# Mixture-of-experts layer on one core: the first block's normalisation on VectorE, unread products around its transposes, setup copies of ScalarE moved, the last turn reordered and stored in halves

## The reference, cut to what matters

```python
xn = layernorm(x)                                   # x: 16 x 512 x 128
q, k, v = xn @ q_w, xn @ k_w, xn @ v_w              # 32 channels
attn = ((q @ k.T) * decay_weights) @ v @ o_w.T * out_scale
logits = xn @ router_w + router_b + load_balancer; rw, sel = softmax(top_2(logits))
e0 = silu(xn @ sw_w1) * (xn @ sw_w3) @ sw_w2
e1 = gelu(sym @ me_c1w + me_c1b) @ me_c2w + me_c2b  # sym: three linear maps of xn
h2 = layernorm(syn + attn_ce); ff = relu(h2 @ f1w + f1b) @ f2w + f2b
e2 = layernorm(h2 + ff) @ gen_w + gen_b
e3 = gelu(xn @ ml_w1 + b) @ ml_w2 + b
out = x + attn + sum(rw * the two experts of sel)
```

## Time and profile before

| | |
|---|---|
| time, median of 3 runs | 475.91 us (475.39 to 476.07) |
| the profiled execution | 475.9 us, its span 474.1 us |
| PE / PEld busy | 456.7 us (96%) / 381.9 us (81%) |
| DVE busy | 389.5 us (82%) |
| ACT / POOL busy | 271.3 us (57%) / 251.8 us (53%) |
| granted TensorE clock, mean | 0.999 |
| HBM traffic | 23 GB/s over the span |

### The profile page before, as it was taken

How to read it: one execution, slowest core, us unless ns; L and a number is a source line. 1 busy time by engine, 2 the same in 40 slices (tenths; PEclk the granted TensorE clock), 3 DMA queues, 4 the chain that set the end, 5 groups by cost and what they waited for, 6 DMA issues and landing times.

```text
span 474.1 us, 9536 instructions
## 1 busy us (share of the span) xinstructions
PE 456.7 (96%) x2892; PEld 381.9 (81%) x2892; DVE 389.5 (82%) x1292; ACT 271.3 (57%) x534; POOL 251.8 (53%) x370
## 2 busy tenths in 40 slices
PE   3879999999999999999999999999999999999994
PEld 2758888897888889788888878878898888878884
DVE  4567988979798897988889798888979888886994
ACT  3582846548284663829457383845728375482831
POOL 4692645737265572726657273664726357471541
PEclk9999999999999999999999999999999999999999
DMA  7300010010101001010000101001010100100000
GB/s 264 18 6 19 2 45 2 1 45 2 46 0 37 7 0 44 0 44 0 21 23 0 44 0 44 0 3 41 0 44 0 44 0 0 44 1 22 3 24 22
DMA packets 18786, 11.43 MB, mean 24 GB/s; under 512 B 1136, under 2 KB 18256, under 8 KB 18768
## 3 DMA queue, kind: packets, MB, share of 16 engines
q1 hardware_dynamic: 18480, 11.20, 8.8%
q10 hardware_dynamic: 288, 0.01, 0.0%
HBM read 6.80 MB, written 4.19 MB: 23 GB/s over the span
## 4 chain that ended last, share of the span: by engine, by line
issue 48%; POOL 36%; POOLq 11%; PE 2%; DVE 1%; ACT 1%; DMA 1%; DVEq 0%
POOL hid3l L430 14%; POOL hidl L434 9%; POOLq L398 7%; POOL n L400 5%; POOL xn L400 5%; POOLq L443 2%; POOLq L396 2%; POOL rstd_u L444 1%; DMA ROW<-rows 1%; POOL negmean_x L395 0%; POOL negmean_c L395 0%; DVE falling L604 0%; PE TR L892 0%; POOL WL L416 0%; ACT hid L523 0%
## 5 line engine op out<-in xcount | busy, mean ns | idle before, releaser
L967 PE MATMUL S<-xh,WH 128*128 128x512 f32 x224 | 98.7, 441 | 2.1 <-ACT hid L523 2.1
L969 PE MATMUL S<-xh,WL 128*128 128x512 f32 x224 | 88.5, 395 | 0.0
L968 PE MATMUL S<-xl,WH 128*128 128x512 f32 x224 | 88.1, 393 | 0.0
L430 POOL TENSOR_TENSOR hid3l<-hid,hid3h 128x512 fp32r<-128x512 f32 x64 | 80.2, 1283 | 0.0
L394 POOL TENSOR_TENSOR veps_x<-mv_x,eps 128x4 f32<-128x4 f32 x16 | 3.2, 199 | 120.9 <-DVE mv_x L582 120.9
L560 ACT ACTIVATE hid<-S,me_b 128x512 f32<-128x512 f32 x32 | 22.1, 689 | 67.4 <-PE S L969 67.3
L925 PE MATMUL EX<-scaled,hid 128*128 128x128 f32 x512 | 59.8, 275 | 0.0
L925 PEld LDWEIGHTS EX<-scaled,hid 128*128 128x128 f32 x512 | 58.4, 192 | 0.0
L967 PEld LDWEIGHTS S<-xh,WH 128*128 128x128 f32 x224 | 42.2, 188 | 18.8 <-issue 3.6
L679 DVE SCALAR_TENSOR_TENSOR OUT<-EX,coef,OUT 128x128 f32<-128x128 f32 x192 | 53.7, 341 | 0.7
L738 DVE SCALAR_TENSOR_TENSOR gate<-th,S 128x512 f32<-128x512 f32 x64 | 43.8, 685 | 8.7 <-ACT th L505 7.8
(11 more groups left out here) (171 smaller groups left out, 1079.2 us busy)
## 6 DMA issues: line engine op xcount, KB each, us to landing
X<-x SPq DMA_DIRECT2D x16, 256.0 KB, 3.0
out<-OUT SPq DMA_DIRECT2D x16, 256.0 KB, 2.4
W<-weights SPq DMA_DIRECT2D x1, 768.0 KB, 8.2
W<-weights SPq DMA_DIRECT2D x1, 512.0 KB, 5.7
W<-weights SPq DMA_DIRECT2D x1, 384.5 KB, 6.7
W<-weights SPq DMA_DIRECT2D x1, 384.0 KB, 6.2
W<-weights SPq DMA_DIRECT2D x1, 192.5 KB, 4.5
W<-weights SPq DMA_DIRECT2D x1, 162.0 KB, 4.4
```

What stands on the lines that cost most here:

```text
L430: pool.tensor_tensor(hid3l[:, j, :], hid[3][:, j, :], hid3h[:, j, :], ALU.subtract) \
L967: pe.matmul(bank[:, :], wh, hi, start=True, stop=False)
L968: pe.matmul(bank[:, :], wh, lo, start=False, stop=False)
L969: pe.matmul(bank[:, :], wl, hi, start=False, stop=True).then_inc(unit_ready, 1)
```

## The change

On DVE `x_moments` of the first group moves ahead of the last two of the ten decay steps. POOL makes only the roots (`root`); DVE normalises the first group's four tiles with four `tensor_scalar`, behind the low half of `ce`. POOL waits for these four before it splits weights. PE gets five products of 64 columns ahead of the first transposes and three of 128 columns behind them, into `ATT`, which nobody reads. The block of setup work of ACT between `c1` and `c2` is taken apart: the four copies of `back` go ahead of `take_x`, the third portion's cast behind the `kv` copies of the first turn, `scaled` behind the copy of `found`. In the last turn PE leaves expert 0 until `u` has been transposed, computes expert 2 first (into `TR`), then expert 0, then expert 1 by tiles (into the four `S` banks). DVE adds the bias of expert 2, computes a product of coefficient and root, adds expert 2, 0 and 1; each tile of expert 1 counts for itself, and SP stores two tiles at a time. Turns 2 to 15 are unchanged.

```diff
@@ -177,6 +177,7 @@
         n1 = sb("n1", [P, NT, P])
         Q = sb("Q", [3 * C, T], F32R)
         K = sb("K", [3 * C, T], F32R)
+        coef_r = sb("coef_r", [P, NT])
         th = sb("th", [P, NT, T])
 
         hid = {e: sb(f"hid{e}", [P, k, T]) for e, k in ((0, 4), (3, 4), (1, 2), (2, 2))}
@@ -245,6 +246,7 @@
         released = [sem(f"released{b}") for b in range(BANKS)]
         x_stats = sem("x_stats")
         x_normed = sem("x_normed")
+        first_root = sem("first_root")
         x_turned = sem("x_turned")
         x_high = sem("x_high")
         x_split = sem("x_split")
@@ -280,6 +282,9 @@
         hid3_low = sem("hid3_low")
         u_turned = sem("u_turned")
         u_read = sem("u_read")
+        last_tile = sem("last_tile")
+        last_step = sem("last_step")
+        last_mixed = sem("last_mixed")
         out_ready = sem("out_ready")
 
         def w(name, first=0, width=None):
@@ -363,9 +368,16 @@
                     sp.wait_ge(att_added, g.count(1, 1))
                     load_x(Group(g.pair, g.off + 2))
 
-            turns(sp, turn, store)
+            def last_store(g):
+                half = NT // 2
+                for n in range(2):
+                    sp.wait_ge(last_mixed, (n + 1) * half)
+                    sp.dma_start(out[g.index()].rearrange("(t p) h -> p t h", p=P)[:, n * half:(n + 1) * half, :],
+                                 OUT[g.par][:, n * half:(n + 1) * half, :]).then_inc(out_stored[g.par], DMA_INC)
+
+            turns(sp, turn, last_store)
             for k in range(2):
-                sp.wait_ge(out_stored[k], DMA_INC * PAIRS)
+                sp.wait_ge(out_stored[k], DMA_INC * (PAIRS + k))
 
 
         @block.gpsimd
@@ -389,12 +401,16 @@
             for e in range(1, E):
                 const(pool.memset(earlier[:, e, 0:e], 1.0))
 
-            def norm(k, src, dst, done):
+            def root(k):
 
                 pool.tensor_tensor(veps[k][:, :], mv[k][:, :, 1], eps4[:, :], ALU.add)
                 pool.tensor_tensor(negmean[k][:, :], mv[k][:, :, 0], minus1[:, :], ALU.mult)
                 pool.drain()
-                pool.tensor_tensor(rstd[k][:, :], veps[k][:, :], nhalf[:, :], ALU.pow)
+                return pool.tensor_tensor(rstd[k][:, :], veps[k][:, :], nhalf[:, :], ALU.pow)
+
+            def norm(k, src, dst, done):
+
+                root(k)
                 pool.drain()
                 for t in range(NT):
                     pool.tensor_scalar(dst[:, t, :], src[:, t, 0:P], negmean[k][:, t:t + 1], rstd[k][:, t:t + 1],
@@ -404,7 +420,8 @@
                 pool.wait_ge(x_stats, g.count(1, 1))
                 norm("x", X[g.par], xn, x_normed)
 
-            norm_x(Group(0, 0))
+            pool.wait_ge(x_stats, 1)
+            root("x").then_inc(first_root, 1)
 
             def low_weights(splits):
 
@@ -415,6 +432,7 @@
                     cols = slice(first_col, first_col + width)
                     pool.tensor_tensor(WL[:, cols], src, WH[:, cols], ALU.subtract).then_inc(split_low, 1)
 
+            pool.wait_ge(x_normed, NT)
             low_weights(range(FIRST_SPLITS))
 
             def turn(g, first, last):
@@ -488,6 +506,10 @@
             act.copy(TH[:, LOGW:TOKW], qkv[:, 3 * C:5 * C]).then_inc(fold_high, 1)
             act.copy(TH[:, 0:P], prod("ce")).then_inc(fold_high, 1)
             high_weights(0)
+            act.wait_ge(pool_const, POOL_CONSTS)
+            act.wait_ge(setup_act, 1)
+            for t in range(NT):
+                act.copy(back[t * C:(t + 1) * C, t * P:(t + 1) * P], oT[:, :]).then_inc(back_laid, 1)
             take_x(Group(0, 0))
             high_weights(1)
             act.wait_ge(w_loaded[LOAD_OF["gen_w"]], DMA_INC)
@@ -509,6 +531,9 @@
                 for t in range(NT):
                     tok, _ = unit(f"tok{t}")
                     act.copy(kv[:, t, :], tok[:, LOGW:TOKW]).then_inc(kv_taken, 1)
+                if first:
+                    for n in range(FIRST_SPLITS, len(WEIGHT_SPLITS)):
+                        high_weights(n)
                 act.wait_ge(qk_ready, g.count(1, 1))
                 act.copy(Q[:, :], qk_bank[0:3 * C, :]).then_inc(qk_high, 1)
                 half_gate(0)
@@ -521,14 +546,6 @@
                 for j in range(4):
                     c, free = unit(f"c{j}")
                     act.activation(hid[3][:, j, :], c[:, :], ACT.Gelu, bias=vec(f"ml_b1{j}")).then_inc(free, 1)
-                    if first and j == 1:
-                        for n in range(FIRST_SPLITS, len(WEIGHT_SPLITS)):
-                            high_weights(n)
-                        act.wait_ge(setup_act, ACT_SETUP)
-                        for t in range(NT):
-                            act.copy(back[t * C:(t + 1) * C, t * P:(t + 1) * P], oT[:, :]).then_inc(back_laid, 1)
-                        act.wait_ge(w_loaded[LOAD_OF["sw_w2"]], DMA_INC)
-                        act.mul(scaled[:, :], w("sw_w2"), 0.5).then_inc(half_done, 1)
                 act.wait_ge(c_turned, g.count(1, 1))
                 act.activation(h2[:, :], TR[:, :], ACT.Identity, bias=vec("n1b"), scale=vec("n1g")) \
                     .then_inc(h2_ready, 1)
@@ -542,6 +559,9 @@
                     act.copy(hid3h[:, j, :], hid[3][:, j, :]).then_inc(hid3_high, 1)
                 act.wait_ge(found_ready, g.count(1, 1))
                 act.copy(found[:, :], ATT[:, 0, :]).then_inc(found_taken, 1)
+                if first:
+                    act.wait_ge(w_loaded[LOAD_OF["sw_w2"]], DMA_INC)
+                    act.mul(scaled[:, :], w("sw_w2"), 0.5).then_inc(half_done, 1)
                 for j in range(2):
                     f, free = unit(f"f1_{j}")
                     act.activation(hid[2][:, j, :], f[:, :], ACT.Relu, bias=vec(f"f1b{j}")).then_inc(free, 1)
@@ -600,13 +620,14 @@
             decay_link(dve.tensor_scalar(falling[:, ZEROTH - 1:ZEROTH], decay[0:1, :], 0.5, 0.5, ALU.mult, ALU.add))
             n = 1
             while n < ZEROTH:
+                if step[0] == DECAY_BEFORE_X:
+                    x_moments(Group(0, 0))
                 more_powers = min(n, ZEROTH - n)
                 decay_link(dve.tensor_scalar(falling[:, ZEROTH - n - more_powers:ZEROTH - n],
                                              falling[:, ZEROTH - more_powers:ZEROTH],
                                              falling[:, ZEROTH - n:ZEROTH - n + 1], None, ALU.mult))
                 n += more_powers
             assert step[0] == DECAY_STEPS
-            x_moments(Group(0, 0))
             taken = [0]
 
             def product(name):
@@ -629,6 +650,10 @@
             product("ce")
             dve.wait_ge(fold_high, 2)
             took(dve.tensor_tensor(TL[:, 0:P], prod("ce"), TH[:, 0:P], ALU.subtract))
+            dve.wait_ge(first_root, 1)
+            for t in range(NT):
+                dve.tensor_scalar(xn[:, t, :], X[0][:, t, :], negmean["x"][:, t:t + 1], rstd["x"][:, t:t + 1],
+                                  ALU.add, ALU.mult).then_inc(x_normed, 1)
             dve.wait_ge(setup_act, 2)
             dve.tensor_tensor(TL[:, P:LOGW], w("router"), TH[:, P:LOGW], ALU.subtract)
             product("ce_b")
@@ -671,10 +696,10 @@
                 took(dve.tensor_tensor(me_b[:, :], prod("me_b", cols=2),
                                        VEC[:, VECS.index("me_c1b0"):VECS.index("me_c1b0") + 2], ALU.add))
 
-            def mix(g, e, added):
+            def mix(g, e, added, count=None):
 
                 dve.wait_ge(ex_ready[e], g.count(1, 1))
-                dve.wait_ge(added, g.count(1, 1))
+                dve.wait_ge(added, g.count(1, 1) if count is None else count)
                 for t in range(NT):
                     ins = dve.scalar_tensor_tensor(out=OUT[g.par][:, t, :], in0=EX[EX_BANK[e]][:, t, :],
                                                    scalar=coef[g.par][:, t, e:e + 1], in1=OUT[g.par][:, t, :],
@@ -845,12 +870,31 @@
                 assert rs[0] == ROUTE_STEPS
 
             def tail(g):
+
                 u_moments(g)
-                expert0(g)
                 u_combine(g)
-                expert1(g)
-                expert2_scale(g)
-                expert2_add(g)
+                dve.wait_ge(ex_taken[3], g.count(1, 1))
+                for t in range(NT):
+                    ins = dve.scalar_tensor_tensor(out=OUT[g.par][:, t, :], in0=gen_bias[:, :],
+                                                   scalar=coef[g.par][:, t, 2:3], in1=OUT[g.par][:, t, :],
+                                                   op0=ALU.mult, op1=ALU.add)
+                ins.then_inc(last_step, 1)
+                dve.wait_ge(u_rstd, g.count(1, 1))
+                dve.tensor_tensor(coef_r[:, :], coef[g.par][:, :, 2], rstd["u"][:, :], ALU.mult).then_inc(last_step, 1)
+                dve.wait_ge(last_step, 2)
+                dve.wait_ge(ex_ready[2], g.count(1, 1))
+                for t in range(NT):
+                    ins = dve.scalar_tensor_tensor(out=OUT[g.par][:, t, :], in0=TR[:, t * P:(t + 1) * P],
```

(60 more changed lines are left out.)

## The result

The changed kernel takes 467.42 us (median of 5 runs, 467.11 to 467.59) against 475.73 us before (5 runs, 475.39 to 476.07). The ratio is 0.9819 with a 95% interval of 0.9805 to 0.9832, so 8.3 us less. Two executions of the later sets, one of 514.02 us (the kernel before with unread products) and one of 2563.41 us (the kernel before), are in the slow state and enter no ratio and no comparison.

The account below looks back on a forecast made before the run. PE was taken to bound the middle, leaving gains at the head and end. From 475.9 us, -0.35 - 2.05 - 2.14 + 0.2 - 1.5 - 0.3 = -6.1 gave 469.8 us (chance 0.55), range 467.9 to 472.3.

Parts of the forecast that it names:

- Part 3: Head, products from `tok` on: run at full instead of half speed, 4.18 to 2.13 us, -2.05 us; bounds all or nothing.
- Part 4: First turn, ahead of `a1`: with ACT's block taken out, PE's stall of 2.14 us goes, -2.14 us.
- The term for `found`: First turn: PE's 0.46 us wait for `found` may grow behind ACT's casts, +0.2 us; bounds 0 and +0.8.
- Part 2: Head, unread products and first transposes: `TR` complete about 12.45 instead of 12.81 us, -0.35 us; bounds -0.05 and -1.1.
- at half speed 0.22: Head: each of the ten records of the five unread products takes 0.22 us, so they run from 9.5 to 11.7.
- My half-speed bound and my "costs nothing" bound: Head, first transposes: gain of 0.05 us if all runs at half speed, 1.1 if the five unread products cost nothing.
- Part 5: Last turn, reordered experts: end at 469.0 instead of 471.34, -2.3 us, cut to -1.5 for DVE and POOL taking turns.
- I take part of it, +0.8: Last turn: bias of expert 2 on DVE and POOL's root exclude each other, costing +0.8 us.
- The halved store: End of the kernel: storing the last 256 KB in two halves saves 0.3 us; bounds 0 and -1.2.
- The low clock at the start: Rival, head: clock stays low until the `tok` products have run, giving 472.1 us; chance 0.15.
- Everything cheaper: Rival: short unread products (-1.1 for -0.35) and no turn-taking at the end (-2.3 for -1.5), 468.2 us; chance 0.13.
- `reach`: Rival, first turn: SP's transfers of `reach` land late, DVE and then PE wait, making the kernel slower; chance 0.02.

## Why the prediction was right or wrong

**The bound and the order of gains: right.** PE sets the pace in the middle, and the turns from e3 on took the same time to 0.13 us. All gains lie where I looked for them.

**Part 3, the clock: right in size** (2.06 for 2.05), but not a certainty: it is right for an early rise. That none of the first five runs was late is luck, as three of five were in each repeat. Against the kernel before on their own chips the repeats are still 8.5 and 8.6 us faster in the median (ratios 0.9815 and 0.9832), so the forecast gain was too small there as well. The kernel without unread products gives the 2 us back in all of its four runs.

**Part 4, ACT's block: right** (2.22 for 2.14), shown by the block put back. In that trace the level fell as well, worth another microsecond; in the kernel before it had not, with the same idle time, so this is no part of the gain measured here. The term for `found` had the wrong sign: +0.2 forecast, -0.3 measured. The wait that shrank stands ahead of L1025 (before) for the state copy: from the record pair ahead of it to L1025 0.80 us pass before, to the same line (L1093) after 0.46. The wait at L1107 stayed. That ACT's work moved ahead made it so is argued, not tested.

**Part 2, the start: the term was mis-sized**, 0.35 for 1.01. The step that failed is "at half speed 0.22" for the unread products. The price per record was right for each level (0.20 to 0.22 in the low-level execution, 0.12 in the profiled one), and in the low-level execution the start came within 0.14 of the forecast (8.35 from the weights, a gain of 0.21). What failed is that I fixed the level at which they run. It is decided anew in each execution, and in the profiled run it rose at 9.3 us, so that the ten records were over at 10.49 and not at 11.7 and the normalised tiles set the transposes. There the earlier moments and DVE's normalisation came through in full, 0.84 us. My half-speed bound and my "costs nothing" bound held it, but the central value did not.

**Part 5, the last turn: mis-sized**, 1.5 for 2.33. The step that failed is "I take part of it, +0.8". The path without turn-taking, 2.3, was right to 0.03. I had carried a 128x16 instruction's wait behind POOL's long subtraction over to POOL's power, a 128x4 instruction. With the bias behind the root the loss was 0.94; beside it, the power merely lasted 0.18 longer. My sign of being right, power and bias one behind the other, didn't show. The Trainium skill's rule ("SBUF — State Buffer", shared port pair) says the loser fully blocks for the whole instruction. That agrees with the subtraction, not with the power: DVE's bias instructions ran on while the power was under way. Where page and trace differ, the trace decides.

**The halved store: 0.47 for 0.3**, borne out by the single store (2.79 against 2.29).

**The rivals.** The low clock at the start is real: with unread products it comes and goes by the execution, and the changed kernel's times reach 470.55; without them it stood in the traced execution, and all four times fit it. "Everything cheaper", 468.2 at 0.13, was the nearest, and it is what happened (1.01 for its 1.1, 2.33 for its 2.3), plus 0.5 us behind `a1`, where I had forecast a loss of 0.2 and 0.3 were gained, and small gains in the other rows. The range was too narrow on this side by 0.5 us: I let it reach to 467.9 though my own best values gave 467.1. `reach` landed in time, as nothing waits for it in the trace; its last transfer was issued up to 12.23, where I had put 13.8.

## What to carry to other kernels

At a kernel's head the price of a TensorE instruction depends on the level that has been reached, and this differs from one execution of the same kernel to the next: look at durations, count the idle times ahead of each stretch, make the forecast for both levels instead of for a mixture, and run the kernel more than once. Keep PE at work from the first moment its operands can exist; products that nobody reads cost little where PE idles anyway, and one gap of 1.6 us behind them can undo them. Before you take a collision of two engines from one pair of instructions over to another, time the new pair: here the 128x512 subtraction held the other engine up to its end and the 128x4 power did not, and which of their differences decides wasn't tested.

## What the runs showed of the hardware that I had not expected

- The clock column reads 1.00 through stretches in which the same record lasts 0.42 us in one execution and 0.27 in another; only durations tell the 1.2 from the 2.4 GHz level.
- With the same head, the level rose at 9.3, 14.6, 15.3 or 18.8 us (the changed kernel twice, then the traces of the single store and of the bias behind the root). The Trainium skill ("TensorE: Matmul & The Clock Gate", Part 1) says that the rise differs from run to run by about half a microsecond; here the spread was 9 us, and the totals of the changed kernel, which go with it where they were traced (467.11 and 467.21 early, 468.40 late), reach from 467.03 to 470.55.
- The level can be lost again within 1.56 us of idling. After 2.14 us it fell about a microsecond after work had resumed in one trace, and stayed in another, of the kernel before.
- An unread product's record takes 0.11 us at the high level at 64 columns as at 128.
- DVE's `tensor_scalar` over a 128x128 tile comes to 0.28 us each (four in 1.12), near the 0.25 that I took and less than POOL's 0.43.
- Turn-taking of DVE and POOL can be long without costing anything: in the changed kernel's first turn the 128x16 coefficient instruction lasted 2.25 us, until POOL's two subtractions ended, and PE never waited for it:

```profile
29.95 2.53 POOL L452 TENSOR_TENSOR hidl<-hid,hidh 128x512 fp32r<-128x512 f32 x2
30.26 2.25 DVE L849 SCALAR_TENSOR_TENSOR coef<-tlean,half 128x16 f32<-128x16 f32 x1
```
